# Transposes in a Mamba block: from TensorE's transpose form to two plain products with the identity, 64 stationary columns each

## The reference

```
proj = x @ in_proj_w.T                      # gate 8192, hBC 8192 + 2*1024, dt 128
hBC  = silu(causal_conv(hBC, conv_w) + conv_b)
hs   = hBC[..., :8192].reshape(b, s, 128, 64)     # 128 heads of 64 channels
dt   = clip(softplus(dt + dt_bias), 0, 100)
...
xch    = hs * dt[..., None]
Y_diag = einsum('bzlhn,bzshn,bhzls,bzshp->bzlhp', C, B, L, xch)
Y      = Y_diag + hs * D
g      = Y * silu(gate)
out    = group_norm(g) * norm_w             # 8 groups of 1024 channels
return out @ out_proj_w.T
```

## Time and profile before

| | |
|---|---|
| median of three runs | 1676.53 us (1674.23 to 1679.68) |
| the profiled execution | 1674.2 us, span 1672.5 us |
| TensorE's products, busy | 1625.8 us, 97% of the span, 9188 instructions |
| TensorE's loads of the stationary operand | 1280.1 us, 77% |
| VectorE | 1177.8 us, 70% |
| ScalarE | 953.0 us, 57% |
| GpSimd | 940.9 us, 56% |
| granted clock of TensorE | 0.993 in the mean |

### The profile page before, as it was taken

The page is one execution under the profiler, slowest core; times in us unless marked ns, Lnnn a source line. Parts: engine busy times, 40 slices in busy tenths (PEclk is TensorE's granted clock), DMA queues, the critical chain, the costliest instruction groups (busy, mean ns, idle before and its releaser), DMA issues.

```text
span 1672.5 us, 25592 instructions
## 1 busy us (share of the span) xinstructions
PE 1625.8 (97%) x9188; PEld 1280.1 (77%) x9188; DVE 1177.8 (70%) x2253; ACT 953.0 (57%) x1584; POOL 940.9 (56%) x714
## 2 busy tenths in 40 slices
PE   8999999999999999999999999999999978889998
PEld 7788888888888888888888888888888855444646
DVE  7767677767876687768675867586858668896443
ACT  6765366546744574558364836483638344995231
POOL 2877568655856595749473948394839462331000
PEclk9999999999999999999999999999999989999999
DMA  5432134212321241224122412241314290000000
GB/s 190 136 115 76 57 104 131 76 57 101 133 73 61 90 137 60 80 89 133 58 88 89 133 57 89 71 134 62 101 57 134 62 162 30 1 15 25 13 14 25
DMA packets 76546, 138.84 MB, mean 83 GB/s; under 512 B 6786, under 2 KB 13954, under 8 KB 76164
## 3 DMA queue, kind: packets, MB, share of 16 engines
q1 hardware_dynamic: 76420, 137.21, 25.8%
HBM read 134.55 MB, written 2.63 MB: 82 GB/s over the span
## 4 chain that ended last, share of the span: by engine, by line
PE 89%; DVE 5%; ACT 2%; issue 1%; DMA 1%; SPq 1%; POOL 0%; DVEq 0%; POOLq 0%; ACTq 0%
PE ps_hs L247 8%; PE ps_hs L249 8%; PE ps_hs L248 7%; PE ps_gate L247 7%; PE ps_gate L248 7%; PE ps_gate L249 7%; PE ps_hs L1148 7%; PE ps_y L1140 7%; PE ps_hs L1149 7%; PE ps_hs L1150 7%; PE ps_gate L1129 4%; PE ps_y L1380 3%; PE ps_hs L1342 3%; PE ps_dec L1342 3%; DVE pr L976 1%
## 5 line engine op out<-in xcount | busy, mean ns | idle before, releaser
L751 DVE SCALAR_TENSOR_TENSOR conv<-ps_hs,cw,conv 128x508 f32<-128x508 f32 (+2 forms) x432 | 320.3, 742 | 30.4 <-ACT conv L516 19.2
L382 POOL TENSOR_SCALAR_AFFINE_SELECT cum_bc<-cum_bc 128x1024 f32<-128x1024 f32 x128 | 139.9, 1093 | 218.1 <-DMA cum_bc<-cum_scratch 217.6
L392 POOL TENSOR_TENSOR cum_bc<-cum_bc,neg_cum 128x1024 f32<-128x1024 f32 x128 | 247.5, 1934 | 10.8 <-POOL cum_bc L382 0.3
L247 PE MATMUL ps_hs<-x_hi,w_hi 128*128 128x512 f32 x576 | 231.5, 402 | 0.0
L247 PE MATMUL ps_gate<-x_hi,w_hi 128*128 128x512 f32 x576 | 224.3, 389 | 2.1 <-DVE xdt L777 2.1
L249 PE MATMUL ps_hs<-x_hi,w_lo 128*128 128x512 f32 x576 | 225.1, 391 | 0.0
L248 PE MATMUL ps_hs<-x_lo,w_hi 128*128 128x512 f32 x576 | 224.2, 389 | 0.0
L248 PE MATMUL ps_gate<-x_lo,w_hi 128*128 128x512 f32 x576 | 224.1, 389 | 0.0
L249 PE MATMUL ps_gate<-x_hi,w_lo 128*128 128x512 f32 x576 | 224.0, 389 | 0.0
L1148 PE MATMUL ps_hs<-wo_hi,g_hi 128*128 128x512 f32 x512 | 202.9, 396 | 8.2 <-DVE acc L941 6.2
L1149 PE MATMUL ps_hs<-wo_lo,g_hi 128*128 128x512 f32 x512 | 200.6, 392 | 0.0
(11 more groups left out here) (146 smaller groups left out, 3216.2 us busy)
## 6 DMA issues: line engine op xcount, KB each, us to landing
cum_bc<-cum_scratch SPq DMA_DIRECT2D x128, 512.0 KB, 4.2
w_raw<-w_in SPq DMA_DIRECT2D x145, 256.0 KB, 4.6
wo_raw<-w_out SPq DMA_DIRECT2D x64, 256.0 KB, 5.0
g_acc<-x_t SPq DMA_DIRECT2D x4, 512.0 KB, 5.5
acc<-x_nat SPq DMA_DIRECT2D x1, 2048.0 KB, 10.1
k_rep<-ctx_t SPq DMA_DIRECT2D x8, 256.0 KB, 11.9
out<-y_out SPq DMA_DIRECT2D x8, 256.0 KB, 2.0
wg_sb<-w_gate SPq DMA_DIRECT2D x1, 1792.0 KB, 12.2
```

Of the source, the lines that this page charges most:

```text
L247: eng.matmul(ps, whi, xhi, start=(k == 0), stop=False)
L392: gp.tensor_tensor(part, part, start.broadcast_to([P, 2, HB, SEQ]), ALU.add).then_inc(S["bc_ok"], 1)
L751: v.scalar_tensor_tensor(out=dst, in0=src, scalar=cw[:, at, TAPS - 1 - n:TAPS - n], in1=dst, op0=ALU.mult, op1=ALU.add).then_inc(S["tap"], 1)
```

## The change

`transposes` no longer issues the transpose form of the product. Each block of 128 by 128 becomes two plain products with the identity as the moving operand: the 64 columns (tokens) `rows` of `hs` are stationary, and the result goes into the same 64 partitions of `ps_gate`. This is the form of the products in `outputs`: 64 stationary columns, 128 moving ones, the halves of the partitions in turn, both operands float32. What lands in `ps_gate` is the same.

```
                 for r in range(2):
                     for b in range(HB):
-                        mm = pe.transpose(ps_gate[r][:, b * P:(b + 1) * P], hs[s % 2][:, r * HB + b, :], ident[:, :])
+                        for e in range(2):
+                            rows = slice(e * SEQ // 2, (e + 1) * SEQ // 2)
+                            mm = pe.matmul(ps_gate[r][rows, b * P:(b + 1) * P], hs[s % 2][:, r * HB + b, rows],
+                                           ident[:, :], start=True, stop=True)
                     mm.then_inc(S["tr_ok"], 1)
```

## The result

The change makes the kernel slower: 1733.59 us (median of 4 runs, 1733.43 to 1734.25) against 1675.92 us before, a ratio of 1.0342 with a 95% interval of 1.0324 to 1.0360. In the profiled executions the span goes from 1672.5 to 1731.7 us, 59.2 us more; the forecast sum was 60.1 us, the predicted time 1736 us. The granted clock is 0.993 in both.

A forecast was written before the change was run, and what follows sets the result against it. TensorE was taken to bound the kernel, so added work adds to the end. Terms of 51.2, 8.6 and 0.3 us made 60.1 us, on the profiled 1674.2 us 1734, as a median 1736 us; range 1727 to 1747 us.

The forecast's parts named there:

- (1): Usual tiles, whose transposes stand right behind the outputs: +0.93 us for each of 55 sets, 51.2 us.
- (2): First tile of a group, behind the products of B and C: +1.23 us, 7 times, 8.6 us.
- (3): Tile 0, at the start: the wait for m_sb covers most of 1.23 us; 0.3 us taken.
- (4): Last tile's set: 0.9 us, covered by TensorE's 3.35 us wait for g_lo, so it costs nothing.
- Who waits: VectorE at L777, multiplying the transposed tile by dt: 0.6 us to spare in the usual tile, so no wait.
- The clock at the end: Last 55 us: if the clock did not fall to half, up to 6.7 us would return; in the range only.
- A: Rival, no loss: each half is a single row, 16 rows at 0.88 us per set; 1682 us; 3%.
- B: Rival, faster: halves of one row each run side by side, 0.44 us per set; 1651 us; 1%.

## Why the prediction was right

**That TensorE sets the time** (97% of the span, 1268.07 of 1270 us busy): held. With 57.9 us more of busy time the span grew by 59.2 us, and twice the work cost in proportion.

**Two rows per plain product**: held exactly, 2048 rows for 1024 halves, and this is the cause of the loss. Whole plain products lose as much, and with one whole row per block, float32 still but of the reduced type, all but 3 us of the loss is gone.

**(1) The usual tile, +0.93 us, 51.2 us**: the run of 64 rows measures 3.64 against the 3.66 us forecast, and from outputs to outputs a tile is 0.91 us longer, so about 50 us. The 0.02 us for leaving the form is not seen in that distance. Alone, the usual sets cost 50.5 us, and 49.6 us in the trace.

**(2) The first tile of a group, +1.23 us, 8.6 us**: 1.96 + 1.90 against 1.87 + 0.79 us, and 0.34 against 0.31 us behind: 1.23 us. Alone, with tile 0, 9.3 us were measured for 8.9, and 8.7 us in the trace without tile 0, for 8.6.

**(3) and (4), the ends**: covered, as the run with the ends alone shows. For (4) the cover is the wait that was named. For (3) the size was near by luck: the prediction named the wait for m_sb, which did not move (0.8 us before and after). The term's 1.23 us went into the wait of the next gates for xdt, 2.1 us before and 0.9 after, which the prediction did not consider at this place.

**Who waits**: VectorE's L777 starts 4.53 us behind the outputs as before (619.48 and 624.01), and has no wait. This is the row, from VectorE's timeline:

```profile
624.01 1.28 DVE L777 TENSOR_TENSOR xdt<-ps_gate,dt_tok 128x512 f32<-128x512 f32 x2
```

**The clock at the end**: fell again, 0.55 from 1420 to 1422 us, behind a wait of 2.45 us; nothing came back. From the start of the outputs ahead of the last tile's transposes to the end of the span it is 322.0 us before (1350.53 to 1672.5) and 322.2 us after (1409.47 to 1731.7). So everything that the change costs lies ahead of there.

**What was wrong is the meaning of one number.** "A row of 64 columns takes 59 ns", and with it "a half costs little more than half of a transpose": a row of a half takes 110 ns, as a whole one does, and two rows run side by side. For the order that the change has, the two readings give the same sum, because the outputs have that order too. That the right price came out of the wrong reading is luck of the order. The two part where the order is another (1734 us by the reading, 1771 measured) and in the rivals. A took single rows of 55 ns one after the other; a float32 pair side by side at 110 ns would cost the same. B took a pair of single rows to last 0.055 us; its 1651 us came near (1656 us), but with 16-bit rows, and no float32 row here is as short. Both were ruled out rightly by the number of rows, but the sentence that set B apart, a pair of outputs taking 0.24 us, counts four rows as a pair; what it should have said is that a pair of rows takes 0.11 us already side by side. Rival A's rule from the Trainium skill (TensorE: Matmul & The Clock Gate, section LDWEIGHTS), that a load's time goes by its columns alone, differs from the trace before, and the measurement decides: a load of 64 columns for the outputs lasts 138 ns, one of 128 for the transposes 140 ns, and one of 128 for the products of B and C 192 ns:

```profile
L1140 PEld LDWEIGHTS ps_y<-m_sb,xdt 128*64 128x64 f32 x2048 | 111.7, 138 | 27.0 <-issue 26.0 <-DVE m_sb L786 1.0
L1129 PEld LDWEIGHTS ps_gate<-ident,hs 128*128 128x128 f32 x512 | 55.2, 140 | 11.0 <-issue 11.0
L1110 PEld LDWEIGHTS ps_dec<-sg,hs 128*128 128x128 f32 x128 | 15.0, 192 | 2.2 <-ACT sg L533 2.2
```

The factor between plain and transpose form, 2.4 in the prediction, is 1.81 / 0.85 = 2.1 in the usual tile. The Trainium skill's direction (Perfetto Trace Analysis, section Transposes) is confirmed. The 4 times of its page TensorE: Matmul & The Clock Gate, section Terms, differ from the 2.1 measured here, and again the measurement decides.

## What to carry to other kernels

Before giving one operation the form of its neighbour, count rows in the trace against instructions in the program: here a float32 product was two rows and a transpose one, and that made nearly all of the 58 us. Price a form by a run of it start to start, and remember that such a price belongs to the order in which it was read. Where an engine is busy for 1268 of 1270 us, its added time is the program's, and only waits such as those at the two ends swallow any; which wait it is, the list of waits of a run tells.

## What the runs showed that was not expected

TensorE starts rows out of the program's order to pair the halves of the array: 2.44 us for 32 rows with four halves of a kind in a row, 1.90 with two, 1.84 in turn, where strictly in order the first would be 3.2 us by estimate. The reach that the traces show is four rows. Halving 128 stationary columns gains next to nothing in either type tried: with the outputs ahead, 3.64 against 3.70 us in float32 and 2.37 against 2.34 us in bf16, and it costs 0.25 to 0.28 us where the form is entered for the set alone. And a 128 by 128 block passes in 55 ns when only its upper 16 bits are read, half of the 106 ns of a float32 transpose. That kernel is 25 us faster than the one before, but it is no replacement: hs keeps 16 of its 32 bits on the way to xdt. Halves in the transpose form, and halves in the reduced float32 type, were not tried.
